# A macaron layer with a grouped state-space mixer: mixing without the zero quarter of each diagonal block

## The reference

```
cs     = cumsum(dt * A)                                # per head, along the chunk
Lmat   = where(tri, exp(cs[l] - cs[s]), 0)             # lower triangle: token l sees s <= l
scores = (C[l] . B[s]) * Lmat
Ydiag  = scores @ (x * dt)
Y      = Ydiag + Yoff + x * D                          # Yoff: the first chunk's state in the second
out    = rmsnorm_by_group(Y * silu(gate)) * norm_w @ out_proj_w.T
```

## Time and profile before

| | |
|---|---|
| median of 3 runs | 1524.92 us (1524.83 to 1527.4) |
| the profiled execution | 1522.31 us |
| its span, first to last instruction | 1520.5 us |
| PE busy | 1477.9 us (97%) |
| DVE / POOL / ACT busy | 1290.9 / 1155.5 / 1015.2 us |
| mean granted clock of TensorE | 0.991 of full speed |

### The profile page before, as it was taken

One profiled execution on the slowest core, in us unless ns is written; L12 is line 12 of the kernel. 1 busy time (PEld: TensorE's weight loads), 2 busy tenths in 40 slices (PEclk: granted clock), 3 DMA queues, 4 the chain that ended last, 5 costly groups with the idle time before them and its releaser, 6 DMA issues. The chain is left out here.

```text
span 1520.5 us, 24373 instructions
## 1 busy us (share of the span) xinstructions
PE 1477.9 (97%) x7720; PEld 1212.3 (80%) x7720; DVE 1290.9 (85%) x1664; ACT 1015.2 (67%) x2154; POOL 1155.5 (76%) x917
## 2 busy tenths in 40 slices
PE   6979899999999999999999999999999999999988
PEld 4767788888888888888888888888888888888766
DVE  6689987998789987998789977998799987998675
ACT  4366777667766777667766677667766777667540
POOL 3017997699958997699959997699859997699830
PEclk9989999999999999999999999999999999999999
DMA  3026542444435442444434442544434442544201
GB/s 126 1 84 193 181 155 89 160 158 149 139 104 160 148 152 84 160 159 154 132 111 156 150 153 77 172 152 151 143 100 162 150 151 74 180 149 141 99 15 56
DMA packets 165680, 198.79 MB, mean 131 GB/s; under 512 B 21040, under 2 KB 86576, under 8 KB 165296
## 3 DMA queue, kind: packets, MB, share of 16 engines
q1 hardware_dynamic: 165552, 197.22, 39.5%
HBM read 160.98 MB, written 36.18 MB: 130 GB/s over the span
## 5 line engine op out<-in xcount | busy, mean ns | idle before, releaser
L166 PE MATMUL bank<-h_hi,mx_w_hi 128*128 128x512 f32 x1152 | 459.4, 399 | 4.4 <-DVE mx_acc L1519 2.8
L167 PE MATMUL bank<-h_lo,mx_w_hi 128*128 128x512 f32 x1152 | 450.3, 391 | 0.0
L168 PE MATMUL bank<-h_hi,mx_w_lo 128*128 128x512 f32 x1152 | 449.7, 390 | 0.0
L976 DVE SCALAR_TENSOR_TENSOR mx_acc<-bank,mx_cw,mx_acc 128x510 f32<-128x510 f32 (+2 forms) x480 | 353.9, 745 | 43.1 <-ACT mx_acc L961 29.9
L1540 DVE TENSOR_TENSOR mx_mix<-mx_mix,mx_cbt 128x1536 f32<-128x1536 f32 x128 | 266.0, 2083 | 37.0 <-ACT mx_mix L1358 37.0
L1348 ACT ACTIVATE mx_mix<-mx_csb,ncs 128x256 f32<-128x256 f32 x512 | 217.9, 498 | 111.1 <-PE bank L1741 109.1
L1232 POOL TENSOR_TENSOR mx_y<-mx_y,mx_sg 128x512 f32<-128x512 f32 x128 | 248.5, 1962 | 19.0 <-DVE mx_y L1548 19.0
L166 PEld LDWEIGHTS bank<-h_hi,mx_w_hi 128*128 128x128 f32 x1152 | 217.4, 189 | 56.0 <-POOL mx_w_lo L920 4.1
L168 PEld LDWEIGHTS bank<-h_hi,mx_w_lo 128*128 128x128 f32 x1152 | 217.1, 188 | 46.4
L167 PEld LDWEIGHTS bank<-h_lo,mx_w_hi 128*128 128x128 f32 x1152 | 217.6, 189 | 42.5
L920 POOL TENSOR_TENSOR mx_w_lo<-mx_w_raw,mx_w_hi 128x512 fp32r<-128x512 f32 x144 | 191.7, 1332 | 74.3 <-ACT mx_w_hi L915 73.8
(11 more groups left out here) (172 smaller groups left out, 2236.8 us busy)
## 6 DMA issues: line engine op xcount, KB each, us to landing
mx_csb<-cs_rows SPq DMA_DIRECT2D x128, 512.0 KB, 4.1
mx_w_raw<-in_w_in SPq DMA_DIRECT2D x144, 256.0 KB, 3.7
x_squares<-mx_th SPq DMA_DIRECT2D x128, 256.0 KB, 2.0
mx_xd<-x_squares SPq DMA_DIRECT2D x512, 64.0 KB, 2.0
mx_wo_raw<-in_w_out SPq DMA_DIRECT2D x64, 256.0 KB, 4.2
res<-in_x SPq DMA_DIRECT2D x8, 256.0 KB, 4.4
out<-res SPq DMA_DIRECT2D x8, 256.0 KB, 2.0
f_base_raw<-in_base_wt SPq DMA_DIRECT2D x1, 1024.0 KB, 7.2
```

The lines of the kernel that those rows point to most:

```text
L166: nc.tensor.matmul(out, w_hi, x_hi, start=first, stop=False)
L167: nc.tensor.matmul(out, w_hi, x_lo, start=False, stop=False)
L168: return nc.tensor.matmul(out, w_lo, x_hi, start=False, stop=last)
L976: self.nc.vector.scalar_tensor_tensor(dst, src[:, :, 0:SEQ - k], self.cw[:, c, TAPS - 1 - k:TAPS - k], dst, ALU.mult, ALU.add).then_inc(s[ ...
```

## The change

The zero quarter is left out of every stage. The 256 query columns of a sequence are put in another order in `mix` and `cbt`: first the 192 queries from 64 on for the first chunk's keys (`FROM0`), then 64 columns which hold two half-height blocks (keys 0 to 63 of the first chunk with queries 0 to 63 on the upper half of the partitions, keys 0 to 63 of the second chunk with its queries 0 to 63 on the lower half), then 64 columns for the second chunk's queries 64 to 127. A row has 320 columns in place of 384.

For the lower half of the partitions to hold the second chunk's first 64 keys, odd token tiles are kept with their halves exchanged: in `transpose_rows` (two products for each odd tile in place of one transpose), in `turn_squares` (two transposes in place of one) and in `b_dot_c` (four products in place of two). The rows of -cs are stored twice in DRAM, in two orders (six stores for two), and `load_cs` loads the upper and lower 64 partitions from one each. POOL copies a set of biases together (`ncs_low`) and makes a constant `limit` of 0 and 1e30.

`mask_first` masks 64 columns in place of 128. `mask_second` becomes a `tensor_tensor` add of `limit`. `decay_from_first` is 192 wide, `decay_from_second` two activations of 64.

`mix_tokens` now does both steps of a pair at once, in four parts: `whole(1)`, `halves(0, 1)`, `whole(0)`, `halves(1, 0)`. `whole(i)` has, for each sequence and head, a product of 192 columns and one of 64 over all 128 keys. `halves(low, high)` has, for each sequence, four products of 64 keys, 64 features and 64 columns, on the four quarters of the array: two heads of one step on the upper rows, two heads of the other step on the lower rows. The last part waits for the second (`half`); `y` is raised by two at the end, and the waits for `mix` and `x_scaled` of both steps stand ahead of the first part.

```diff
+HC = CH // 2
+FROM0 = SEQ - HC
+PAIR = FROM0 + CH
...
             def load_cs(g, st):
                 step_slot_freed(sp, s["decay"], g, st)
-                src = ncs_dram[g, st // 2, :, st % 2, :].partition_broadcast(P)
-                sp.dma_start(csb[:, st % 2, :, :], src).then_inc(cs_in[st % 2], 16)
+                for v in range(2):
+                    src = ncs_dram[v, g, st // 2, :, st % 2, :].partition_broadcast(HC)
+                    sp.dma_start(csb[v * HC:(v + 1) * HC, st % 2, :, :], src).then_inc(cs_in[st % 2], 16)
...
-                nc.gpsimd.affine_select(out=mix[:, st % 2, :, :, :].rearrange("p h b l -> p (h b) l")[:, :, SEQ:PAIR],
-                                        in_=rows_of(st)[:, :, CH:SEQ], compare_op=ALU.is_ge, fill=MASKED,
-                                        base=0, pattern=[[0, 2 * HB], [1, CH]],
-                                        channel_multiplier=-1).then_inc(s["masked1"], 1)
+                rows = rows_of(st).rearrange("p r (k l) -> p r k l", l=HC)[:, :, 0:4:3, :]
+                nc.gpsimd.tensor_tensor(mix[:, st % 2, :, :, FROM0:PAIR].rearrange("p h b (k l) -> p (h b) k l", k=2), rows,
+                                        m.limit[:, :, :].unsqueeze(1).to_broadcast([P, 2 * HB, 2, HC]),
+                                        ALU.add).then_inc(s["masked1"], 1)
...
-                    nc.tensor.matmul(banks[b][:, 0:SEQ], bb[:, 0:CH], cc, start=True, stop=True)
-                    last = nc.tensor.matmul(banks[b][:, SEQ:PAIR], bb[:, CH:SEQ], cc[:, CH:SEQ],
+                    c1, c2 = FROM0, FROM0 + HC
+                    nc.tensor.matmul(banks[b][:, 0:c1], bb[:, 0:CH], cc[:, HC:SEQ], start=True, stop=True)
+                    nc.tensor.matmul(banks[b][0:HC, c1:c2], bb[:, 0:HC], cc[:, 0:HC], start=True, stop=True)
+                    nc.tensor.matmul(banks[b][0:HC, c2:PAIR], bb[:, CH + HC:SEQ], cc[:, CH + HC:SEQ], start=True, stop=True)
+                    last = nc.tensor.matmul(banks[b][HC:CH, c1:PAIR], bb[:, CH:CH + HC], cc[:, CH:SEQ],
                                             start=True, stop=True)
...
+            def halves(low, high):
+
                 for b in range(HB):
                     c0 = b * SEQ
                     for hd in range(2):
                         rows = slice(hd * HD, (hd + 1) * HD)
-                        nc.tensor.matmul(Y_BANK[i][rows, c0:c0 + SEQ], xd[:, i, rows, 2 * b],
-                                         mix[:, i, hd, b, 0:SEQ], start=True, stop=False)
+                        nc.tensor.matmul(Y_BANK[low][rows, c0:c0 + HC], xd[0:HC, low, rows, 2 * b],
+                                         mix[0:HC, low, hd, b, FROM0:FROM0 + HC],
+                                         start=low == 0 and b == 0, stop=low == 1 and b == HB - 1)
                     for hd in range(2):
                         rows = slice(hd * HD, (hd + 1) * HD)
-                        last = nc.tensor.matmul(Y_BANK[i][rows, c0 + CH:c0 + SEQ], xd[:, i, rows, 2 * b + 1],
-                                                mix[:, i, hd, b, SEQ:PAIR], start=False, stop=True)
-                last.then_inc(s["y"], 1)
+                        last = nc.tensor.matmul(Y_BANK[high][rows, c0 + CH:c0 + CH + HC], xd[HC:CH, high, rows, 2 * b + 1],
+                                                mix[HC:CH, high, hd, b, FROM0:FROM0 + HC],
+                                                start=False, stop=high == 0 and b == HB - 1)
+                return last
+
+            def whole(i):
+
+                for b in range(HB):
+                    c0 = b * SEQ
+                    for hd in range(2):
+                        rows = slice(hd * HD, (hd + 1) * HD)
+                        nc.tensor.matmul(Y_BANK[i][rows, c0 + HC:c0 + SEQ], xd[:, i, rows, 2 * b],
+                                         mix[:, i, hd, b, 0:FROM0], start=i == 1 and b == 0, stop=False)
+                    for hd in range(2):
+                        rows = slice(hd * HD, (hd + 1) * HD)
+                        nc.tensor.matmul(Y_BANK[i][rows, c0 + CH + HC:c0 + SEQ], xd[:, i, rows, 2 * b + 1],
+                                         mix[:, i, hd, b, FROM0 + HC:PAIR], start=False, stop=False)
+
+            def mix_tokens(g, j):
+
+                x_scaled(pe, g, 2 * j + 1)
+                pe.wait_ge(s["mix"], 1 + STEPS * g + 2 * j + 2)
+                if j == 0:
+                    pe.wait_ge(s["cbt"], 1 + 2 * g + 1)
+                pe.wait_ge(s["ysb"], 1 + STEPS * g + 2 * j)
+                whole(1)
+                halves(0, 1).then_inc(s["half"], 1)
+                whole(0)
+                pe.wait_ge(s["half"], PAIRS * g + j + 1)
+                halves(1, 0).then_inc(s["y"], 2)
```

More of the change, by code:

```diff
@@ L53 @@
 PAIRS = XT
-PAIR = SEQ + CH
+HC = CH // 2
+FROM0 = SEQ - HC
+PAIR = FROM0 + CH
 NE, RANK = 8, 16
@@ L82, in place_constants @@
     m.dtt = sb("dtt", [P, TT, NH])
+    m.ncs_low = sb("ncs_low", [P, TT // 2, NH])
+    m.limit = sb("limit", [P, 2, HC])
     m.stat = sb("stat", [P, TT, 6])
@@ L716, in gpsimd @@
         nc.gpsimd.memset(self.ones[:, :], 1.0).then_inc(s["iota"], 1)
+        nc.gpsimd.memset(self.m.limit[:, :, :], 0.0).then_inc(s["iota"], 1)
+        for n, at, step in ((3, slice(0, HC), 0), (4, slice(HC, CH), HC)):
+            rows = self.m.limit[at, :, :]
+            pool.wait_ge(s["iota"], n)
+            nc.gpsimd.affine_select(out=rows, in_=rows, compare_op=ALU.is_ge, fill=MASKED, base=0,
+                                    pattern=[[step, 2], [1, HC]], channel_multiplier=-1).then_inc(s["iota"], 1)
+        pool.wait_ge(s["iota"], 5)
         pool.wait_ge(s["w_hi"], 1)
@@ L723, in gpsimd @@
             self.ip.remainder_w(pool, 0, w)
+        for h in range(2):
+            pool.wait_ge(s["kept"], 2 * h + 1)
+            for rows, t in ((slice(0, HC), 0), (slice(HC, CH), 1)):
+                tiles = self.m.ncs[rows, 4 * h:4 * h + 4, :].rearrange("p (b k) h -> p b k h", k=2)
+                pool.wait_ge(s["iota"], 5 + 2 * h + t)
+                nc.gpsimd.tensor_copy(self.m.ncs_low[rows, 2 * h:2 * h + 2, :], tiles[:, :, t, :]).then_inc(s["iota"], 1)
     def round_weights(self, act):
@@ L810, in transpose_rows @@
         for src, bank in ((self.ncs, 4), (self.dt, 6)):
-            for t in range(4):
-                last = nc.tensor.transpose(m.bank[bank + h][:, t * NH:(t + 1) * NH],
-                                           src[:, h, t * P:(t + 1) * P], m.ident[:, :])
+            for t in range(0, 4, 2):
+                nc.tensor.transpose(m.bank[bank + h][:, t * NH:(t + 1) * NH], src[:, h, t * P:(t + 1) * P], m.ident[:, :])
+            for t in range(1, 4, 2):
+                for c in range(2):
+                    last = nc.tensor.matmul(m.bank[bank + h][(1 - c) * HC:(2 - c) * HC, t * NH:(t + 1) * NH],
+                                            src[:, h, t * P + c * HC:t * P + (c + 1) * HC], m.ident[:, :],
+                                            start=True, stop=True)
             last.then_inc(s["tr"], 1)
@@ L883, in __init__ @@
             "tap", "conv", "mix", "xd", "sg", "ysb", "cbt", "gsum", "outsb", "ms", "inv", "wolo",
-            "yg", "ylo", "ssum", "wlo", "masked0", "masked1", "rows", "base_in", "a_in", "lb_in"])
+            "yg", "ylo", "ssum", "wlo", "masked0", "masked1", "rows", "half", "base_in", "a_in", "lb_in"])
         self.raw_in = [ctx.enter_context(nc.semaphore(f"mx_raw_in{i}")) for i in range(3)]
@@ L1356, in decay_from_second @@
                     for hd in range(2):
-                        tile, head = 2 * (HB * hf + b) + 1, GH * g + 2 * j + hd
-                        last = nc.scalar.activation(mix[:, i, hd, b, SEQ:PAIR], mix[:, i, hd, b, SEQ:PAIR], ACT.Exp,
-                                                    bias=m.ncs[:, tile, head:head + 1], scale=-1.0)
+                        pair, head = HB * hf + b, GH * g + 2 * j + hd
+                        low, second = mix[:, i, hd, b, FROM0:FROM0 + HC], mix[:, i, hd, b, FROM0 + HC:PAIR]
+                        nc.scalar.activation(low, low, ACT.Exp, bias=m.ncs_low[:, pair, head:head + 1], scale=-1.0)
+                        last = nc.scalar.activation(second, second, ACT.Exp,
+                                                    bias=m.ncs[:, 2 * pair + 1, head:head + 1], scale=-1.0)
                 last.then_inc(s["decay"], 1)
@@ L1785, in pair @@
                         project_out(g, p)
-                for st in steps:
-                    mix_tokens(g, st)
+                mix_tokens(g, j)
             def tail(g, more):
@@ L1823, in program @@
         ffn_phase(nc, m, "f1", x, None, base_wt, router_wt, lora_a, lora_b,
-                  dt_of=(w_dt, dt_bias, ncs_dram.rearrange("g j h f n -> (g j h) (f n)"), ip))
+                  dt_of=(w_dt, dt_bias, [ncs_dram[v].rearrange("g j h f n -> (g j h) (f n)") for v in range(2)], ip))
         mixer_phase(nc, m, ip, norm_w, w_out, ncs_dram, x_dram, last_ln, sums, early)
```

33 lines of the change are left out of this document (16 added, 17 removed).

## The result

The changed kernel takes 1598.28 us in the median of 4 runs (1597.16 to 1598.74), against 1525.66 us of the kernel before beside it: a ratio of 1.047 [1.046, 1.049]. The profiled execution has a span of 1596.4 us, 75.9 more than the 1520.5 before.

The account below looks back on a forecast made before the run. PE was taken as the bound; mixing +66, C.B +17, ahead of the mixer +2 and group 0 -4 sum to +81 us on 1522.3, 1603, and 1605 us as median; range 1530 to 1668, the forecast's own 1585 to 1625.

Parts of the forecast that it names:

- PE is the bound, one for one: In nearly all of the mixer, what PE gains or loses is the kernel's gain or loss.
- Pace of short passes, 0.11; whole sequence 0.55: Mixing: weight loads hold a 64-column pass to 0.11 us; a sequence of whole products takes 0.55, four 2.22.
- Rival 3: 64-wide loads take half a 128-wide one and hide, so short passes stream at 0.055: 1542 us, chance 0.10.
- Quarters, 0.11 a set: Mixing's quarter products: four run at once, one load of 0.11 us a set, 8 sets, 0.88 us a pair.
- Rival 1: Quarters run in turn, row halves sharing one path: a set takes 0.22 us, +56, 1661 us, chance 0.12.
- Changes of shape, 0.2 each: Mixing: changes of the array's shape go from 2 a pair to 5, at 0.2 us each.
- Rival 2: Changes between 128x64, 64x64 and full shape cost nothing new: -51, 1554 us, chance 0.15.
- C.B, +0.52 a sequence: C.B: a sequence goes from 0.66 us to 1.17, +0.52, times 32 sequences +17 us.
- The others hidden: PE at some 20.5 us a pair hides ACT +1.25, DVE -0.5 and POOL +0.7 us a pair.
- Ahead of the mixer, +2: Before the mixer: more stores, POOL copies and longer products in transpose_rows cost +2 us (0 to 4).
- 4.3 us of room: Mixing: last xd ready at 507.85, PE wants it at 512.15, room for 1.3 + 1.25 + 0.7 us of delay.
- Group 0, -4: First pairs of group 0: PE's idle 6.6 us takes up part of the loss, -4 us (-6.6 to 0).

Follow-up runs that it names:

- experiment 3: The changed kernel (strided operand) with the mixing parts ordered whole(1), whole(0), halves(0,1), halves(1,0), three changes of shape in place of five: 1598.34 us.
- experiment 1: The changed kernel with scale_x writing out of place into y, so that the mixing's stationary operand is contiguous: 1539.76 us.
- experiment 7: As experiment 1, with b_dot_c doing both sequences' 192-column products first and load_w(3) ahead of load_cs: 1539.19 us.
- experiment 6: As experiment 1, but with two token tiles interleaved, so that the stationary operand's features lie 8 bytes apart: 1542.03 us.
- experiment 4: The kernel before, with y raised by two after the second step's mixing in place of one after each: 1524.21 us.
- experiment 2: The kernel before with the contiguous stationary operand of experiment 1 in its mix_tokens: 1518.51 us.
- experiment 5: The changed kernel (strided operand) with 128 moving columns in place of 64 in each quarter product, every product starting its own sum: 1603.13 us.

## Why the prediction was right

The forecast of 1605 us is 7 us, 0.4%, above the result. Its terms, by stretch, against the two profiled executions:

| stretch | predicted | measured |
|---|---|---|
| 51 full pairs | 51 x 1.03 = 52.5 | 51 x 0.97 = 49.5 |
| 7 pairs with a tail | 7 x (1.03 + 4 x 0.52) = 21.8 | 7 x 1.90 = 13.3 |
| ahead of the first mixing | 2 + 4 x 0.52 = 4.1 | 125.06 - 119.45 = 5.6 |
| pairs 0 to 3 of group 0 | 4 x 1.03 - 4 = 0.1 | 74.87 - 72.03 = 2.8 |
| last two mixings and the end | 2 x 1.03 = 2.1 | 4.7 |
| sum | 80.6 | 75.9 |

The sum is nearer than its terms. The first two rows are 11.5 us too high, the last three 6.8 too low, and that these partly cancel is luck. What the prediction rests on, the pairs and PE's pace in them, came as it said.

- **PE is the bound, one for one:** right. Pair and PE's busy time are both 20.42.
- **Pace of short passes, 0.11; whole sequence 0.55:** right as a size: 677.50 - 676.94 = 0.56 in experiment 3, where whole sequences follow one another unhindered. The reason was only half right. The loads do set the pace, but by their 16-byte step. The prediction compared the first load at the 64-wide shape, of `xd`, with that at the 128-wide shape, of `w_hi`, found both 0.1, and took a load's cost to be the same at either width. It had compared a strided load of 64 columns with a contiguous one of 128. Its second row, L577 in the earlier trace rows, was read wrongly: of the 0.32 us of the four loads the last one's own 0.14 is a part, so that they start (0.32 - 0.14) / 3 = 0.06 apart, not 0.08:

```profile
L577 PEld LDWEIGHTS bank<-ident,f_lt x16: 133/136/138, 24.4 to 1497.2; 16*128 16x128 f32 x16
```

  These loads are contiguous (slices of `lt`), so the fast pace stood in the trace of the kernel before. Rival 3, short loads at 1542, is in effect experiment 1, at 1539.8. The Trainium skill (TensorE: Matmul & The Clock Gate, LDWEIGHTS), columns / 1.2 or 53 ns for 64, agrees with the contiguous sets at 0.06 and not with the strided ones at 0.12.
- **Quarters, 0.11 a set:** 0.12. Rival 1 (rows in turn, 0.22) is out by the starts 0.01 us apart.
- **Changes of shape, 0.2 each:** somewhat less. What remains of the mixing is 4.00 - 4 x 0.56 - 8 x 0.12 = 0.80, 0.16 for each of five; experiments 3 and 7 give 0.15 and 0.13 for those taken away. Rival 2 (nothing) is out. The supposed half of it that is the exposed load did not shrink with the contiguous operand: 3.04 - 4 x 0.44 - 8 x 0.06 = 0.80 again.
- **C.B, +0.52 a sequence: the term that was mis-sized.** It measured (1.90 - 0.97) / 4 = 0.23, by which 32 sequences cost 7.4 us in place of 17. The price of 0.11 a pass was carried over from `xd` to `acc`, where the operand is contiguous and a pass takes 0.06.
- **The others hidden:** right in all full pairs. Sizes: ACT +56.7 / 64 = 0.89 a pair for 1.25, DVE -0.70 for -0.5, POOL +23.5 / 64 = 0.37 for 0.7, `mask_second` 1.30 as read. Before its exps of 192 columns ACT now waits 250 us in all for the late `y` (109 before its exps of 256), and no full pair is longer for it: idle time off the critical path.
- **Ahead of the mixer, +2:** too low, 5.6. Some 2 us of it is a wait that the prediction knew of and took to be covered by 4.3 us of room: the first product of a mixing now needs the scaled `xd` of both steps. At the first mixing there is no such room. PE waits 2.26 us for POOL, whose second `xd` is ready at 125.01, the first at 123.04; in the kernel before, PE began at 119.45, behind the first one. The changed kernel's PE and POOL, then POOL of before:

```profile
125.06 0.44 PE L1781 MATMUL bank<-mx_mix,mx_xd 128*64 128x192 f32 x2 [2.26 <-POOL mx_xd L1280]
121.99 1.05 POOL L1280 TENSOR_TENSOR mx_xd<-mx_xd,mx_gdt 128x512 f32<-128x512 f32 x1 [0.74 <-DMA mx_xd<-x_squares]
123.97 1.04 POOL L1280 TENSOR_TENSOR mx_xd<-mx_xd,mx_gdt 128x512 f32<-128x512 f32 x1 [0.93 <-DMA mx_xd<-x_squares]
```

```profile
117.88 1.27 POOL L1253 TENSOR_TENSOR mx_xd<-mx_xd,mx_gdt 128x512 f32<-128x512 f32 x1 [1.25 <-DMA mx_xd<-x_squares]
```

  The first `xd` itself is 3.9 us later. Some 2 of these arise before the mixer's first projection, which starts at 101.95 in place of 99.93; where the rest comes from stays open. POOL's second copy of biases (96.02 to 96.88) is among the last steps of the phase, and then four `csb` loads hold SP's queue for 2.59 us where two took 0.88. The prediction named the two issues but counted them at nothing. The weight's load behind them goes out 3.3 us later (101.17 against 97.87), but that this delays the start is not shown: in experiment 7 it goes out at 96.33 and in experiment 6 at 100.37, and their first mixings start at 122.93 and 123.19.
- **Group 0, -4:** did not come; the stretch grew by 2.8. PE's idle time there stayed, 74.87 - 68.08 = 6.8 us for 6.6, since the masks, exps and `y` that PE waits for came later as well. That reason is argued, not tested.
- **The end, not foreseen beyond its two mixings.** The windows of the stretch between the starts of the last two mixings, in the kernel before, in experiment 4, in the changed kernel and in experiment 3:

```profile
1420.95:1433.81 12.86, 11.65 (x69) 9.23 (x69) 7.91 (x7) 10.51 (x25) 10.41 (x8) 1.00 0.18 54
```

```profile
1420.56:1433.99 13.43, 11.61 (x70) 9.23 (x69) 7.58 (x6) 10.50 (x25) 10.34 (x8) 1.00 0.19 60
```

```profile
1492.13:1508.20 16.07, 14.10 (x102) 11.33 (x101) 7.36 (x7) 10.97 (x32) 14.10 (x11) 0.89 0.16 49
```

```profile
1492.20:1508.26 16.06, 12.49 (x101) 10.04 (x100) 8.11 (x8) 11.56 (x33) 13.94 (x11) 1.00 0.15 49
```

  The stretch is 3.2 us longer than before. Its own mixing accounts for 0.97. The rest is time in which PE is held up, by its waits in the trace for POOL. With no projection left to cover it, PE waits 1.97 us for POOL's split of the previous `y` (0.48 before). Behind that wait the granted clock, the last column but two, is 0.50, the 1.2 GHz level:

```profile
1503.67 0.80 PE L170 MATMUL bank<-mx_wo_hi,mx_yt_hi 128*128 128x512 f32 x1 [1.97 <-POOL mx_yt_lo L1264]
```

```profile
1504.00:1506.00 2.00, 2.00 (x6) 1.52 (x6) 2.00 (x1) 2.00 (x5) 2.00 (x2) 0.50 0.00 0
```

  The twelve products of 512 columns that follow take 4.5 us up to the mixing, some 1.5 longer than in the kernel before, and yet the low clock is not what the stretch costs. In experiment 3 PE waits as long, the clock stays at 1.00, and the stretch is the same, since PE then waits once more, for POOL's `xd`:

```profile
1503.76 0.50 PE L170 MATMUL bank<-mx_wo_hi,mx_yt_hi 128*128 128x512 f32 x1 [2.01 <-POOL mx_yt_lo L1264]
...
1508.26 0.44 PE L1781 MATMUL bank<-mx_mix,mx_xd 128*64 128x192 f32 x2 [1.48 <-POOL mx_xd L1280]
```

  In the changed kernel the slow products only fill that second wait. POOL works there from 1496.12 on without a pause, through two masks of twice the length, two gates, two splits and both `xd`; before, PE went on behind the first `xd`. POOL's `xd` of before, then of after:

```profile
1432.71 1.05 POOL L1253 TENSOR_TENSOR mx_xd<-mx_xd,mx_gdt 128x512 f32<-128x512 f32 x1
```

```profile
1504.81 3.30 POOL L1280 TENSOR_TENSOR mx_xd<-mx_xd,mx_gdt 128x512 f32<-128x512 f32 x2
```

  This account is read from the traces; only the late release was run by itself.

Why the change loses even with the good layout is then a sum from experiments 1 and 2. In a pair, the columns that are left out are worth 4 x 0.65 - (4 x 0.44 + 8 x 0.06) = 0.36 us, where the prediction had 0.44 for them. Three more changes of shape take 0.45 to 0.48. The mixing comes out at 3.04 against 2.94, the pair at 19.43 against 19.35. But that is the smaller part. The two profiled executions lie 26.7 us apart (the medians 21.2): by the starts of their mixings 5.7 ahead of the first, 4.8 in pairs 0 to 3 of group 0, 7.8 in the seven tails, 4.7 from the last mixing but one to the end, and only 3.8 in the 51 full pairs. With experiment 3's order a pair would be some 0.02 to 0.03 shorter, by an estimate from the rows of experiment 3; that was not run.

## What to carry to other kernels

Here, leaving out columns was worth 0.36 us a pair, less than the changes of shape that the pieces brought, and far less than the 1.0 us by which short passes exposed a slow weight load. So, before products are cut shorter, look at how far apart each stationary operand's columns lie in memory: a stride that long passes hide is exposed by short ones. And look at both ends of the program by themselves: a wait that has room in every full pair had none at the first mixing and at the last. Take the price of a pass or a load from a row with the same layout, not only the same shape: this prediction was right on the mixing because its row was of `xd` itself, and wrong by more than half on C.B, where it was not.

## What the runs showed of the hardware

- Sets of products with stationary operands of 64 fp32 columns follow one another at 0.06 us with the columns 4 or 8 bytes apart, and at 0.12 us with 16; there the weight load is the pace (experiment 5).
- Four 64x64 quarters, on two halves of the rows and two of the columns, start within 0.02 us and run side by side.
- A change between the shapes 128x128, 128x64 and 64x64 cost 0.13 to 0.16 us.
- A wait on TensorE for its own last product, with nothing between, cost 0.27 us.
- Behind a wait of 1.97 us near the end TensorE's granted clock was 0.50; behind one of 2.01 us at the same place, in experiment 3, it was 1.00.
